# Attention heads on one core: a score maximum and an exponential taken earlier in each period

## The reference

```python
k = x @ W_lat + b_lat                                   # (2, 512, 128)
q = (x @ W_d + b_d).reshape(2, 512, 16, 128).transpose(0, 2, 1, 3)
att = einsum('bhtl,bsl->bhts', q, k) / sqrt(128)
att = softmax(where(causal, att, -inf), axis=-1)
y = einsum('bhts,bsl->bhtl', att, k)
x = layernorm(x + concat_heads(y) @ W_proj + b_proj)
scores = x @ router_weight + router_bias                # the best 256 of 512 tokens
h = gelu(x[best] @ w1 + b1) @ w2 + b2
x = layernorm(2 * x + scatter(h * sigmoid(scores[best])))
```

## Time and profile before

| | us |
|---|---|
| median of 3 runs | 309.45 |
| lowest, highest | 309.11, 309.55 |
| the profiled execution, own time | 309.75 |
| its span, first to last instruction | 307.9 |
| TensorE busy | 290.8 (94%) |
| VectorE busy | 229.6 (75%) |
| ScalarE busy | 211.8 (69%) |
| GpSimd busy | 147.0 (48%) |

### The profile page before, as it was taken

One profiled execution on the slowest core, in us unless ns is written; L12 is line 12 of the kernel. 1 busy time (PEld: TensorE's weight loads), 2 busy tenths in 40 slices (PEclk: granted clock), 3 DMA queues, 4 the chain that ended last, 5 costly groups with the idle time before them and its releaser, 6 DMA issues.

```text
span 307.9 us, 6338 instructions
## 1 busy us (share of the span) xinstructions
PE 290.8 (94%) x1962; PEld 262.5 (85%) x1962; DVE 229.6 (75%) x698; ACT 211.8 (69%) x585; POOL 147.0 (48%) x202
## 2 busy tenths in 40 slices
PE   7999999999999999999999998999999999985991
PEld 4878999999999999999998797788999999875990
DVE  2678777777777777778888878977887775886574
ACT  3688777777777777777776785686877777541632
POOL 3557433333333485555575564577583111672021
PEclk9999999999999999999999999999999999998998
DMA  6591111111111111111111111111100000000013
GB/s 192 103 326 48 35 36 34 34 34 34 34 34 34 34 35 36 34 38 34 34 36 34 35 36 35 35 26 44 27 19 27 21 0 0 3 0 2 0 35 104
DMA packets 17739, 13.44 MB, mean 44 GB/s; under 512 B 1433, under 2 KB 17458, under 8 KB 17714
## 3 DMA queue, kind: packets, MB, share of 16 engines
q1 hardware_dynamic: 17714, 13.13, 14.8%
HBM read 12.07 MB, written 1.05 MB: 43 GB/s over the span
## 4 chain that ended last, share of the span: by engine, by line
PE 78%; DVE 12%; ACT 4%; issue 2%; SPq 1%; DMA 1%; POOLq 0%; DVEq 0%; ACTq 0%
PE bank L358 15%; PE bank L360 14%; PE bank L359 14%; PE bank L457 10%; PE ps_out L358 5%; PE ps_out L359 5%; PE ps_out L360 5%; PE bank L507 2%; PE bank L437 2%; DVE ties L1055 1%; DVE sel L1034 1%; DVE probs L891 1%; DVE beats L1050 1%; DVE pT_lo L898 1%; PE bank L545 1%
## 5 line engine op out<-in xcount | busy, mean ns | idle before, releaser
L714 ACT ACTIVATE probs<-probs,negmax 128x512 f32<-128x512 f32 (+3 forms) x128 | 72.6, 575 | 13.1 <-DVE negmax L891 11.8
L1158 POOL TENSOR_TENSOR wd_hi<-wd_raw,zero 128x256 fp32r<-128x256 f32 x32 | 23.8, 743 | 95.0 <-DVE probs L941 89.0
L721 ACT CAST pT_hi<-bank 128x512 fp32r<-128x512 f32 (+2 forms) x96 | 43.5, 488 | 32.7 <-PE bank L457 32.7
L891 DVE CUSTOM_DVE_ANT_0 probs<-bank,mask_row 128x512 f32<-128x512 f32 (+3 forms) x128 | 59.1, 481 | 0.6 <-PE bank L360 0.6
L898 DVE TENSOR_TENSOR pT_lo<-bank,pT_hi 128x512 fp32r<-128x512 f32 (+2 forms) x96 | 52.8, 551 | 7.3 <-ACT pT_hi L721 7.2
L457 PE MATMUL bank<-ident,probs 128*128 128x128 f32 x320 | 45.7, 273 | 2.1 <-DVE pT_lo L898 2.1
L457 PEld LDWEIGHTS bank<-ident,probs 128*128 128x128 f32 x320 | 37.9, 140 | 9.7 <-DVE pT_lo L898 4.2
L358 PE MATMUL ps_out<-wp_hi,yT_hi 128*128 128x256 f32 x128 | 38.7, 302 | 0.1
L358 PE MATMUL bank<-kT_hi,qT_hi 128*128 128x512 f32 (+2 forms) x96 | 37.6, 392 | 0.2 <-DVE qT_lo L845 0.2
L906 DVE TENSOR_TENSOR yT_lo<-bank,yT_hi 128x512 fp32r<-128x512 f32 x32 | 22.1, 690 | 20.1 <-PE bank L360 14.0
L360 PE MATMUL ps_out<-wp_hi,yT_lo 128*128 128x256 f32 x128 | 36.1, 282 | 0.0
(11 more groups left out here) (146 smaller groups left out, 763.2 us busy)
## 6 DMA issues: line engine op xcount, KB each, us to landing
wd_raw<-in_L_attn_W_d SPq DMA_DIRECT2D x32, 128.0 KB, 2.2
wp_raw<-in_L_attn_W_proj SPq DMA_DIRECT2D x32, 128.0 KB, 2.1
wf_raw<-in_L_ffn_w SPq DMA_DIRECT2D x2, 1024.0 KB, 7.3
x_nat<-in_L_attn_x SPq DMA_DIRECT2D x4, 256.0 KB, 3.1
out<-x SPq DMA_DIRECT2D x3, 256.0 KB, 3.1
out<-x SPq DMA_DIRECT2D x2, 128.0 KB, 1.9
wlat_raw<-in_L_attn_W_lat SPq DMA_DIRECT2D x1, 128.0 KB, 3.5
bproj_all<-in_L_attn_b_proj SPq DMA_DIRECT2D x1, 128.0 KB, 3.4
```

The lines of the kernel that those rows point to most:

```text
L714: act.activation(p_tile(s, j), p_tile(s, j), ACT.Exp, bias=negmax[:, s, j:j + 1], scale=-1.0, accum_out=sums[:, s, j:j + 1]).then_inc(exp_ ...
L721: act.copy(pT_hi[:, turns[n][3]], turns[n][2]).then_inc(pt_hi_done, 1)
L891: dve.tensor_tensor_reduce(p_tile(s, j), score_bank[j], mask_row[:, (TILES - 1 - j) * P:], -SCALE, -MASKED, ALU.add, ALU.min, accum_out=ne ...
L1158: pool.tensor_tensor(hi, src, nothing, ALU.add).then_inc(hi_done, 1)
```

## The change

On VectorE, a period now begins with a memset of one column (`begun`, a new tile that nothing reads), which carries the wait for tile 3's scores; then comes the maximum of tile 3, and behind it `yT_lo`. The maximum of tile 2 moves from behind the first `pT_lo` to a place ahead of the early piece, and the wait for tile 2's scores moves up with it. On ScalarE, the exponential of tile 3 moves from behind the two casts of the turned probabilities to a place ahead of them. TensorE, GpSimd and SyncE keep their order. The maxima of tiles 1 and 0, and all behind them, keep theirs.

```diff
+        begun = sb("begun", [P, 1])
...
+                if at.live(0):
+                    exps(at, (3,))
                 if at.live(-1):
                     wait(act, y_ready, p - 1)
                     turned(at, 0)
...
                 if at.live(0):
-                    exps(at, (3, 2))
+                    exps(at, (2,))
...
                 if at.live(0):
                     wait(dve, scores_ready, p * 3 + 1)
+                if at.live(0):
+                    dve.memset(begun[:, :], 0.0)
+                    maxima(at, (3,))
+                    wait(dve, scores_ready, p * 3 + 2)
                 if at.live(-2):
                     wait(dve, y_hi_done, p - 1)
                     dve.tensor_tensor(yT_lo[:, :], ps_y[:, :], yT_hi[:, :].bitcast(F32),
                                       ALU.subtract).then_inc(y_lo_done, 1)
                 if at.live(0):
-                    maxima(at, (3,))
+                    maxima(at, (2,))
                 early_piece(at)
-                if at.live(0):
-                    wait(dve, scores_ready, p * 3 + 2)
                 if at.live(-1):
                     turned(at, 0)
                 if at.live(0):
-                    maxima(at, (2,))
                     wait(dve, scores_ready, p * 3 + 3)
```

## The result

| | before | after |
|---|---|---|
| median, us | 309.45 (308.99 to 310.79, 9 executions) | 311.67 (310.66 to 313.9, 9 executions) |
| ratio | | 1.0064, 95% interval 1.0036 to 1.0093 |
| profiled execution, own time | 309.75 | 310.66 |
| its span | 307.9 | 308.9 |

The change makes the kernel 0.64% slower. The forecast of 310.2 had the sign and missed the size, and 311.67 lies outside its range of 308.5 to 311.4. The profiled execution of after is the fastest of its nine. The others fall into two groups by their mean granted TensorE clock: three more at 0.990 or 0.991 with 310.68 to 311.08, and five at 0.981 or 0.982, four of them with 311.67 to 311.82 and one with 313.9. Before's nine executions have no clock on record, except the profiled one (309.75 at 0.991).

What follows compares the result with a forecast made beforehand. TensorE's own list was taken to bound plain periods, leaving early-piece periods and period 1 to matter. Lost 2.87, won 1.5 and 0.5, gives 0.87, taken as 0.7 us slower: 310.2 us, range 308.5 to 311.4.

Steps and rivals of the forecast that it cites:

- the sum: Whole kernel: 2.87 us lost, less 1.5 and 0.5 won, is 0.87 slower, taken as 0.7.
- term of -0.5 for period 23: VectorE, period 23: the last of three comparisons should come behind GpSimd's weight splits and run shorter, 0.5 us off.
- Plain periods: Periods without extra pieces: TensorE is busy throughout, so the change costs 0 and gains 0.
- The memset's step: VectorE, head of a plain period: the added one-column memset takes 0.08 us ahead of tile 3's maximum.
- the slack: Plain periods: time by which the first `pT_lo` ends before delaying TensorE's third turn, shrinking from 0.55 us to 0.04.
- Period 1: Period 1: the values wait 0.65 us for the last `pT_lo`, which comes about 0.3 us earlier.
- the heads: Starts of periods 21, 22, 24 and 25: TensorE's waits for late VectorE work go, 1.2 us won together.
- the third turn's waits: Early-piece periods: TensorE waits longer for the first `pT_lo`, behind memset and tile 2's maximum; 2.87 us lost.
- Pieces beside the splits: VectorE's early pieces, slow beside GpSimd's weight splits: most still fall inside them; other than period 23's, either way.
- E: Early-piece periods: length from the piece's start to `pT_lo`'s start; third-turn delay goes from E - 1.06 to E - 0.50.
- the first rival: Plain periods: a longer chain to `pT_lo` makes each one pay the excess, 312.8 or 319 us; chance 0.14.
- The rival of the pieces slipping free: Early pieces: four or more of some ten contended instructions escape GpSimd's splits, 0.5 to 1.5 us faster; chance 0.14.

Runs made afterwards that it cites:

- the 14 matmuls: 14 128x512 matmuls on zeros added in TensorE's idle time ahead of batch entry 1's ranking: changed kernel 309.29 us, kernel before 307.62 (again 307.61).
- the kernel of 310.55: Kernel before with the 14 matmuls and the early pieces moved directly behind the first low part; 310.55 us.
- the kernel of 305.85: Changed kernel without added matmuls, early pieces moved behind the first low part, ScalarE's order as before; 305.85 us, ratio 0.9876 to the kernel before.

## Why the prediction was wrong

The step that failed is the base of the sum with its term of -0.5 for period 23: the gain was counted against a profile that held the longer form of that period, and most executions of before don't have it. Behind it come a tail whose clock the sum left out, and prices of single pieces that were off both ways.

Right were:

- **Plain periods.** No gain, no loss. The memset's step, taken at 0.08, is 0 and the first low part came 0.18 earlier than forecast (124.88 for 125.06); of that 0.09 is the step from the cast to the low part, 0.60 where it waits for one semaphore (124.28 to 124.88) and 0.69 where it waited for two. So the slack is about 0.2 us and not 0.04.
- **Period 1**, 0.31 won for a forecast 0.3 (the same without ScalarE's part), and **the heads**: 0.12, 0.15, 0.27 and 0.59 won in periods 21, 22, 24 and 25, 1.13 for a forecast 1.2. The weight loads did run less far ahead there: the first turn's began 0.18 us ahead of its first matmul in a plain period of before (122.99 and 123.17) and 0.03 in period 24 (194.01 and 194.04).
- **Where the loss is**: the third turn's waits in periods 18 to 27, with tile 2's maximum as the main cause, by the experiment that moved it back. The memset's share of the forecast is nothing.

Against its own profile the sum came near: 0.87, against 1.06 us between the heads. Part of that is luck. The third turns are 2.47 us later, where 2.87 less 0.5 had been forecast, but by period the errors go both ways: 20 lost 0.28 for 0.56, 21 and 24 lost 0.47 and 0.60 for 0.92 together, 18 and 19 0.13 for 0.27, 26 0.76 for 0.56, 27 0.32 for nothing, and 23 won 0.09 for a forecast loss of 0.06.

Wrong were:

- **The base.** The sum was made against one profiled execution, 309.75, and its period 23 of 8.79 was the larger of two sizes. The term "period 23's last comparison slips from GpSimd's splits, -0.5" counted as a gain of the change what most executions of before already have. No run with after's whole VectorE order shows that slip: the last comparison took 0.82 in all four profiles, as before. What ran short is the middle one, 0.41 where it was 0.92, beside a split of 0.93 where that was 0.74, and period 23 is 8.72: that is 0.07 under the larger size and 0.5 over the smaller. With the 14 matmuls, where the clock is out of it, 1.67 us was measured for 0.7 forecast, and this term is the larger part of the gap of 0.97. The hint was there: 309.75 against a median of 309.45 was noted and passed over. Of before's 22 later executions at 0.990 or 0.991, 20 lie at 308.78 to 309.25 and two at 309.74 and 309.90.
- **The rounding.** 0.87 was lowered to 0.7 for steps "taken at their upper end". The memset's step was; the sizes of the pieces were not.
- **Pieces beside the splits.** They were beside GpSimd's splits before and after, and met them otherwise. Period 26's piece took 1.55 us to the low part for 1.28, and the `selT` piece of period 27 took 0.99 us by its row where E was put under 0.5 (its row was 0.48 before); period 20's took 1.27 for 1.47. The remark that it "may go either way by part of a split" was right; it belonged in the sum's bounds with its numbers.
- **The tail.** The prediction had no term for it. Of the 2.2 us between the two medians 1.67 is the order of work; the rest is, as far as can be told without before's clocks, how many executions of each nine fell to the slower clock. Before has that group too: of its 60 executions beside the experiments 29 had 0.980 or 0.981 (309.68 to 310.51) and 22 had 0.990 or 0.991 (308.78 to 309.90). After had it in 7 of 15. At equal clock the two kernels differ by about 1.8 us at either level (medians 310.85 and 309.09; 311.69 and 309.88). That 311.67 lies over the range at all is chance of this mix: the next six executions of the same kernel had 311.08, inside it.

In signs: the first rival, plain periods losing their slack, didn't happen. It does happen with ScalarE's part alone, at 17.7 us, by a maximum that waits for `yT_lo` and not by the memset. The rival of the pieces slipping free happened to one instruction of some ten. Its sum was wrong as well: 0.87 + 0.5 - 1.9 to - 2.4 is 0.5 to 1.0 us faster and not 0.5 to 1.5.

What stays open: which of the two lengths the low clock takes, what decides the length of the first comparison in period 23, the middle clock of 0.986 in nine executions of before, and two single long executions, 313.9 of after and 312.82 of the kernel of 310.55. The one profile at 0.986 (the kernel of 305.85, 305.53 us) has the length of 6.8 us, but 1.5 us of it fell into the idle time, where the one at 0.981 has 0.7.

## What to carry to other kernels

Ahead of a result that the busiest engine waits for, no side work should stand: the pieces moved behind it gain 4.7 us in the one order. But look at what else the moved work then stands ahead of, since in the other order the same move lost 2.9, and one place further on made 5 us of difference. What an order is worth depends on its surroundings: VectorE's part of the change loses 1.7 us with the pieces ahead of the low part and gains 1.7 with them behind it, and ScalarE's part costs between nothing and 17.7. Before a sum is made from one profile, set its own time against the median: a profile 0.3 us off can hold an instruction that took the rarer, longer of its lengths (0.85 us for 0.28), and its long row then turns up in the sum as a gain.

## What the runs showed of the hardware

- A one-column memset that carries a wait costs nothing that shows: its row of 0.06 us lies inside that of the next instruction, and 32 of them moved the median by 0.1 us or less.
- Two instructions of VectorE and GpSimd whose recorded starts differ by 0.03 to 0.06 us took two lengths from one profile to the next: 0.28 or 0.85 us for the comparison, 0.82 or 0.73 for the split beside it, and 0.6 us of the period (8.22 or 8.80).
- Around the end of 3.4 us of idle time TensorE's granted clock went to 0.50, for 3.4 us in some profiles and 6.8 in others, and matmuls of 128x256 started 0.21 us apart rather than 0.12; the groups of times that go with it are about 0.8 us apart. With 14 matmuls of 128x512 in the idle time the clock stayed at 1.00 there, the slower group was gone, and the times lay 1.5 us under the faster one.
